# A graph-attention layer: edge weights multiplied into the gathered rows instead of into the one-hot matrices

## The reference, cut to what matters

```
z = (x @ W).reshape(n, HEADS, ODIM)
el = jnp.sum(z * al, axis=-1)
er = jnp.sum(z * ar, axis=-1)
e = jax.nn.leaky_relu(el[src] + er[dst], negative_slope=NEG_SLOPE)
e_max = jax.ops.segment_max(e, dst, num_segments=n)
ex = jnp.exp(e - e_max[dst])
denom = jax.ops.segment_sum(ex, dst, num_segments=n)
alpha = ex / denom[dst]
msg = z[src] * alpha[:, :, None]
out = jax.ops.segment_sum(msg, dst, num_segments=n)
out = out + x.reshape(n, HEADS, ODIM)
out = out + b.reshape(HEADS, ODIM)
out = jax.nn.elu(out)
```

## Time and profile before

| what | value |
|---|---|
| runs | 4824.91, 4829.48, 4825.26 us (median 4825.26) |
| the profiled execution, its span | 4824.0 us |
| PE matmul busy | 3342.4 us, 69% of the span |
| POOL busy | 2537.5 us, 53% |
| DVE busy | 2350.8 us, 49% |
| ACT busy | 1279.2 us, 27% |
| PE's granted clock in both GAT layers | about 0.5 of full speed |

### The profile page before, as it was taken

The page is one execution under the profiler, slowest core; times in us unless marked ns, Lnnn a source line. Parts: engine busy times, 40 slices in busy tenths (PEclk is TensorE's granted clock), DMA queues, the critical chain, the costliest instruction groups (busy, mean ns, idle before and its releaser), DMA issues. The chain is left out here.

```text
span 4824.0 us, 104766 instructions
## 1 busy us (share of the span) xinstructions
PE 3342.4 (69%) x33932; PEld 2406.6 (50%) x33933; DVE 2350.8 (49%) x7219; ACT 1279.2 (27%) x4694; POOL 2537.5 (53%) x2630
## 2 busy tenths in 40 slices
PE   6567766676667775677777776666576776767676
PEld 4334444444444444455555555555455555555555
DVE  6445444444544444445444444444344554444455
ACT  5112211212212212233333333323222222222232
POOL 6444444444444443555555555553655555555553
PEclk9777777777777777555555555555555555555555
DMA  7222222222222222333333333332333333333332
GB/s 231 78 79 83 78 75 80 80 79 81 81 78 81 77 80 84 88 99 94 94 98 93 98 96 94 96 94 75 96 93 102 94 94 94 97 99 93 94 93 82
DMA packets 241750, 442.92 MB, mean 92 GB/s; under 512 B 83665, under 2 KB 134933, under 8 KB 241567
## 3 DMA queue, kind: packets, MB, share of 16 engines
q0 software_dynamic: 119808, 334.13, 25.4%
q1 hardware_dynamic: 121887, 108.14, 7.3%
HBM read 381.95 MB, written 60.10 MB: 92 GB/s over the span
## 5 line engine op out<-in xcount | busy, mean ns | idle before, releaser
L1655 POOL DMA_INDIRECT nodes<-z_rows,scratch x1664 | 1644.4, 988 | 1272.8 <-issue 415.7
L1101 POOL DMA_INDIRECT scratch<-h_rows,scratch x832 | 818.8, 984 | 941.7 <-DVE nodes L1251 716.0
L1732 PE MATMUL ge_part<-nodes,scratch 128*32 128x64 f32 x13312 | 472.6, 313 | 243.2 <-DVE scratch L1927 133.5
L1624 ACT COPY scratch<-ge_part 128x260 f32<-128x260 f32 x208 | 78.3, 376 | 1851.5 <-remote 1665.8
L1145 PE MATMUL ce_part<-nodes,scratch 128*32 128x128 f32 (+1 forms) x6656 | 456.7, 394 | 126.2 <-issue 113.4
L1732 PEld LDWEIGHTS ge_part<-nodes,scratch 128*32 128x32 f32 x13312 | 359.4, 167 | 296.5 <-issue 153.2
L1145 PEld LDWEIGHTS ce_part<-nodes,scratch 128*32 128x32 f32 x6656 | 256.5, 140 | 331.5 <-issue 279.2
L1279 DVE TENSOR_TENSOR nodes<-nodes,ce_sum 128x512 f32 x105 | 72.3, 689 | 707.6 <-remote 367.0
L1737 PE MATMUL ge_part<-scratch 128*32 128x4 f32 x3328 | 209.9, 200 | 261.5 <-issue 259.3
L1746 PE MATMUL ge_sum<-scratch 128*128 128x128 f32 x832 | 243.6, 445 | 208.4 <-ACT scratch L1624 208.2
L1919 DVE TENSOR_TENSOR scratch<-scratch,ge_runs 128x32 f32<-128x32 f32 x208 | 44.0, 212 | 692.4 <-remote 675.5
(11 more groups left out here) (269 smaller groups left out, 5802.1 us busy)
## 6 DMA issues: line engine op xcount, KB each, us to landing
nodes<-z_rows,scratch POOLq DMA_INDIRECT x1664
nodes<-hT SPq DMA_DIRECT2D x56, 256.0 KB
scratch<-h_rows,scratch POOLq DMA_INDIRECT x832
z_rows<-scratch SPq DMA_DIRECT2D x28, 264.0 KB
z_rows<-nodes SPq DMA_DIRECT2D x28, 264.0 KB
hT<-scratch SPq DMA_DIRECT2D x28, 256.0 KB
hT<-nodes SPq DMA_DIRECT2D x28, 256.0 KB
nodes<-x_rows SPq DMA_DIRECT2D x28, 256.0 KB
```

The lines of the kernel that those rows point to most:

```text
L1101: nc.gpsimd.indirect_dma_start(xg[u][:, i * D:(i + 1) * D], None, m.h_rows, bass.IndirectOffsetOnAxis(ap=idx[r][:, k:k + 1], axis=0)).then ...
L1655: nc.gpsimd.indirect_dma_start(zg[r][:, k * ZW:(k + 1) * ZW], None, m.z_rows[layer], bass.IndirectOffsetOnAxis(ap=idx[r][:, k:k + 1], axis ...
L1732: ins = nc.tensor.matmul(ps_part[j * TW:(j + 1) * TW, h * HF:(h + 1) * HF], weighted(k, h), zg[r][:, k * ZW + h * HF:k * ZW + (h + 1) * HF ...
```

## The change

The numerators are written where the gathered row keeps el, which has been read by then: the exponential goes straight into columns 256 to 259 of each tile of `zg[r]`. The 256 columns of each row are then multiplied in place by the row's numerators, head by head: DVE takes the even tiles in one instruction of 1024 elements to a partition and tile 1 in another of 256; ACT takes tiles 3, 5 and 7 in 12 instructions of 64 elements. One matmul per tile then sums 260 columns with the plain one-hot. The buffers `hots` and `ex` go, and with them the waits for `part_summed` (v + 4: the sums of the step before are done with `hots`) ahead of the weighting on DVE and ACT.

```diff
-                nc.scalar.activation(ex[u], diff[u], ACT.Exp).then_inc(ex_ready, 1)
+                nc.scalar.activation(numerators(r), lanes(diff[u]), ACT.Exp).then_inc(ex_ready, 1)
...
-                act.wait_ge(part_summed, v + 4)
                 act.wait_ge(ex_ready, v * 2 + 2)
-                for k in range(G // 2 + 1, G, 2):
+                for k in range(3, G, 2):
                     for h in range(HEADS):
-                        ins = nc.scalar.activation(weighted(k, h), one_hot(r, k), ACT.Copy,
-                                                   scale=ex[u][:, h * (G + 1) + k:h * (G + 1) + k + 1])
-                ins.then_inc(hots_act_ready, 1)
+                        at = k * ZW + D + h
+                        ins = nc.scalar.activation(head_rows(r, k, h), head_rows(r, k, h), ACT.Copy,
+                                                   scale=zg[r][:, at:at + 1])
+                ins.then_inc(rows_act_ready, 1)
...
-                for h in range(HEADS):
-                    for j in range(NB):
-                        k = 2 * j + q
-                        ins = nc.tensor.matmul(ps_part[j * TW:(j + 1) * TW, h * HF:(h + 1) * HF], weighted(k, h),
-                                               zg[r][:, k * ZW + h * HF:k * ZW + (h + 1) * HF],
-                                               start=(q == 0 and h == 0), stop=(q == 1), skip_group_check=True)
                 for j in range(NB):
                     k = 2 * j + q
-                    ins = nc.tensor.matmul(ps_part[j * TW:(j + 1) * TW, D:D + HEADS], one_hot(r, k),
-                                           lanes(ex[r % 2])[:, k, :], start=False, stop=(q == 1), skip_group_check=True)
+                    ins = nc.tensor.matmul(ps_part[j * TW:(j + 1) * TW, 0:D + HEADS], one_hot(r, k),
+                                           zg[r][:, k * ZW:k * ZW + D + HEADS], start=(q == 0), stop=(q == 1),
+                                           skip_group_check=True)
...
+            def scale_rows(r, first, last):
+
+                by_tile = zg[r].rearrange("p (k w) -> p k w", w=ZW)[:, first:last:2]
+                rows = by_tile[:, :, 0:D].rearrange("p k (h f) -> p k h f", h=HEADS)
+                by = by_tile[:, :, D:D + HEADS].rearrange("p k (h o) -> p k h o", o=1)
+                return V.tensor_tensor(rows, rows, by.broadcast_to([P, len(range(first, last, 2)), HEADS, HF]), ALU.mult)
...
                 dve.wait_ge(ex_ready, v * 2 + 1)
-                dve.wait_ge(part_summed, v + 4)
-                weighted_one_hots(r, 0)
-                weighted_one_hots(r, 1).then_inc(hots_ready, 1)
+                scale_rows(r, 0, G).then_inc(rows_scaled, 1)
                 if ahead >= 1:
                     over_tiles(v + 1, 1 - u)
                 scale_first(v - 1, 1 - u, base)
-                weighted_one_hots(r, 0, 1).then_inc(hots_ready, 1)
+                scale_rows(r, 1, 2).then_inc(rows_scaled, 1)
```

More of the change, by code:

```diff
@@ L1405, in gat_stage @@
         hot = [scratch(G * TW) for r in range(4)]
-        hots = scratch(G * HEADS * TW)
         hotT = scratch(2 * P)
@@ L1425, in gat_stage @@
         diff = [scratch(LANES) for u in range(2)]
-        ex = [scratch(LANES) for u in range(2)]
         node = Mem()
@@ L1463, in gat_stage @@
          er_ready, raw_ready, score_ready, eT_ready, ends_ready, lv_ready, state_ready, ini_ready, init_ready, fwd_ready,
-         max_ready, maxT_ready, diff_ready, ex_ready, hots_ready, hots_act_ready, half_summed, part_summed, sums_ready, scaled,
+         max_ready, maxT_ready, diff_ready, ex_ready, rows_scaled, rows_act_ready, half_summed, part_summed, sums_ready, scaled,
          summed, added) = [
@@ L1468, in gat_stage @@
                              "eT_ready", "ends_ready", "lv_ready", "state_ready", "ini_ready", "init_ready", "fwd_ready",
-                             "max_ready", "maxT_ready", "diff_ready", "ex_ready", "hots_ready", "hots_act_ready",
+                             "max_ready", "maxT_ready", "diff_ready", "ex_ready", "rows_scaled", "rows_act_ready",
                              "half_summed", "part_summed", "sums_ready", "scaled", "summed", "added")]
@@ L1480, in one_hot, with numerators, head_rows @@
             return hot[r][:, at:at + TW]
-        def weighted(k, h):
-            at = (k * HEADS + h) * TW
-            return hots[:, at:at + TW]
+        def numerators(r):
+            return zg[r].rearrange("p (k w) -> p k w", w=ZW)[:, :, D:D + HEADS]
+        def head_rows(r, k, h):
+            at = k * ZW + h * HF
+            return zg[r][:, at:at + HF]
         @block.sync
@@ L1722, in tile_sums @@
             def tile_sums(v, r, q):
-                pe.wait_ge(hots_ready, v * 2 + (q + 1))
+                pe.wait_ge(rows_scaled, v * 2 + (q + 1))
                 if q == 0:
@@ L1727, in tile_sums @@
                 else:
-                    pe.wait_ge(hots_act_ready, v + 1)
-                for h in range(HEADS):
-                    for j in range(NB):
-                        k = 2 * j + q
-                        ins = nc.tensor.matmul(ps_part[j * TW:(j + 1) * TW, h * HF:(h + 1) * HF], weighted(k, h),
-                                               zg[r][:, k * ZW + h * HF:k * ZW + (h + 1) * HF],
-                                               start=(q == 0 and h == 0), stop=(q == 1), skip_group_check=True)
+                    pe.wait_ge(rows_act_ready, v + 1)
                 for j in range(NB):
                     k = 2 * j + q
-                    ins = nc.tensor.matmul(ps_part[j * TW:(j + 1) * TW, D:D + HEADS], one_hot(r, k),
-                                           lanes(ex[r % 2])[:, k, :], start=False, stop=(q == 1), skip_group_check=True)
+                    ins = nc.tensor.matmul(ps_part[j * TW:(j + 1) * TW, 0:D + HEADS], one_hot(r, k),
+                                           zg[r][:, k * ZW:k * ZW + D + HEADS], start=(q == 0), stop=(q == 1),
+                                           skip_group_check=True)
                 return ins
```

## The result

The changed kernel takes 4772.64 us (median of 4 runs, 4756.19 to 4807.04) against 4825.09 us: a ratio of 0.9889, 95% interval 0.9847 to 0.9932. It is faster, by 52 us where 295 were forecast. The profiled execution is the slowest of the four, with a span of 4805.3 us: in it the untouched stages ahead of layer 0 took 31 us longer than in the profile before (the first gather of `z_rows` comes at 1934.71 us, before at 1904.05), and from there to the end it is 49 us shorter.

A forecast was written before the change was run, and what follows sets the result against it. Bound: lock-step of POOL's gathers and PE's sums. A step falls from 13.55 to 12.2 us (9.77 of gathers plus a gap); 208 x 1.40 = 291 us off 4824.0 gives 4530 us; range 4190 to 4815, likeliest case 4375 to 4640.

The forecast's parts named there:

- the lock-step of POOL's trains and PE's sums: GAT step: POOL waits for the sums, which are not seen done while POOL issues gathers; 13.5 us per step.
- L1624 at 2628.19 to L1732 at 2632.33 is 4.1 us, plus 0.4 of DVE: Way from ACT's copy to the even half: 4.5 us, so it starts at 2642.2, amid the second four gathers.
- The gap is 2.09 us as now or 2.73 as in the late step: POOL's gap behind eight gathers, read from a present train and one whose second odd gather came late: step 11.9 to 12.5 us.
- 12.2: Forecast time in us of one GAT step, the middle of 11.9 to 12.5, against 13.55 before.
- with 16 instructions I expect ...: Odd half, 16 PE instructions instead of 80: counts as done about 1.2 us after its start, releasing POOL early.
- the lock-step stays: Rival: a half ending inside a block of gathers is held however short it is; 4780 to 4825 us, or 4805; chance 0.16.
- POOL alone is the bound: Rival: neither half is held and POOL never waits; 4105 to 4295 us, most likely 4230; chance 0.24.
- The multiply holds up POOL: Rival, slower: DVE's longer row multiplies stretch or block POOL's gathers; 4908 us, or 5160 for the whole multiply; chance 0.08.
- 0.11 us is all that one multiply cost a gather: Argument against the slower rival: the gather beside the third L1927 takes 1.06 us instead of 0.95.
- The cited queue of 64 entries: TensorE's queue: 80 instructions wait for room, 16 don't; were it the cause, the even half would not be held either.

The follow-up runs named there:

- control: The changed kernel itself, run again on chip 5: 4645.71 us, 0.9832 of the kernel before.
- e1: The changed kernel with the sums of a half in 20 matmuls instead of 4, same columns: 4748.76 us, 1.0039 of the kernel before.
- e7: The changed kernel without the row multiplication but for 2 numbers of each head and one ScalarE activation: 4596.38 us, 0.9723 of the kernel before.
- e12: The kernel before with a POOL pause of 512 numbers ahead of the third gather of each four: 4723.28 us, 0.9986 of the kernel before.
- e8: The changed kernel with each gather replaced by a direct DMA of the same size from fixed places: 3980.73 us, 0.8421 of the kernel before.
- e4: The changed kernel with POOL filling 1024 unused numbers ahead of every four odd gathers: 4566.91 us, 0.9671 of the kernel before.
- e2: The changed kernel with a half's sums in 8 matmuls, 32 instructions instead of 16: 4682.53 us, 0.9896 of the kernel before.

## Why the prediction was wrong, by its own steps

The bound was read rightly: the lock-step of POOL's trains and PE's sums. So were the new pieces: VectorE's multiply 1.21 to 1.23 us (1.21 forecast), ScalarE's 12 activations 2.97 (3.0), the four matmuls 1.10 (1.2), and ScalarE was never late for the odd half in the timelines shown. The odd half counts as done 1.17 us after its start (1.2), and POOL went on without a gap to the eighth gather in 77 of 88 steps of layer 0. A slip of names changed nothing: the four gathers that the prediction calls odd (from 2635.90) are released by the even half and are the even ones.

**The step that failed is "L1624 at 2628.19 to L1732 at 2632.33 is 4.1 us, plus 0.4 of DVE", and with it "The gap is 2.09 us as now or 2.73 as in the late step".** The 4.5 us from ACT's copy to the even half is right for the step that it was read from, r = 2 (4.5 measured), and was taken for all four. That is the one place of a quad in layer 0 that has no work on the nodes in its way. In the other three there is some (in layer 0 PE has a node matmul at r = 0, 2 and 3, three steps of a quad and not two), and the prediction put it at nothing. In the kernel before it cost nothing: the way took 3.3 to 4.1 us on average at every r, and this work fell into the time in which the sums were held anyway. The control shows the way with r = 1, where PE's result is seen at once (L1692 ends at 2638.59):

```profile
2635.58 0.38 ACT L1626 COPY scratch<-ge_part 128x260 f32<-128x260 f32 x1 [6.40 <-issue]
...
2638.74 0.47 DVE L1887 TENSOR_TENSOR_SCAN scratch<-scratch,ge_eT 36x128 f32<-36x128 f32 x1 [2.24 <-PE ge_eT L1692]
...
2639.45 0.67 DVE L1954 TENSOR_TENSOR ge_node<-nodes,ge_node 128x512 f32<-128x512 f32 x1
...
2640.14 0.87 DVE L1957 SCALAR_TENSOR_TENSOR nodes<-nodes,bias,ge_node 128x256 f32<-128x256 f32 x2
...
2640.93 0.68 DVE L1963 COPY nodes<-nodes 128x768 f32 x1
...
2641.54 1.21 DVE L1923 TENSOR_TENSOR nodes<-nodes 128x1024 f32<-128x1024 f32 x1
...
2642.80 1.09 PE L1733 MATMUL ge_part<-nodes,scratch 128*32 128x260 f32 x8 [1.15 <-DVE nodes L1923]
```

7.2 us without any hold, of which VectorE's work on the nodes takes 2.1. In the first comparison a hold of what comes ahead of it is added in 13 of 22 quads (L1692 in the step shown), up to 11.8 us. Where the way is that long, the even half falls behind the train instead of into it, and the gap grows to 3.4 and 5.4 us in layer 0. The gaps of 2.09 and 2.73 us were read at r = 2 and r = 3, and there it measured 2.8 and 1.9.

In numbers, 12.2 was 9.77 us of gathers and a gap of 2.4. In layer 0 the mean gap is 3.4 (1.0 more), in layer 1 it is 2.3, as forecast. The gathers are 0.3 us longer per step in layer 0 and 0.6 in layer 1. Some 0.3 to 0.4 us more go to a gap that is left ahead of the odd four at r = 0 and to the late second gather at r = 2, which the kernel before has too. That makes 13.6 and 13.1: 1.4 and 0.9 us of the forecast gain gone. What each piece of the nodes' work costs no run with it left out shows; that it stands in the way is read from the timelines.

What makes a half held was said as a hunch ("with 16 instructions I expect ..."), and e1 bears it out. I counted PE's MATMUL and LDWEIGHTS records from the start of a train to each result whose consumer is seen waiting, and call it late when the consumer starts over 0.6 us behind the record's end. In the changed kernel 3 of 516 with fewer than 35 records ahead were late, 89 of 106 with 35 to 45, and all 144 with more. There the place would do as well: under 5 us into the train 1 of 514 was late. In the kernel before, all 364 with 70 or more were late, from 1.6 us into the train on, and 20 of 24 with 35 to 45; so it is not the place. But the count isn't sharp either: L1692 is held 4.65 us with 38 records ahead (2646.81), and seen in 0.13 with 42 in another step (2350.59). In e1, 89 of 226 with fewer than 35 were late: after a short gap things are held sooner. It is the instructions since PE was last well supplied, as far as I can tell. A step has some 96 such records (4747 MATMUL and as many loads in the 98.75 steps of the layer 0 window). Had I made the count before, it would have shown that a part of them must be held in a train of eight.

Of the rivals, "the lock-step stays" is nearest in time (4805) and wrong in mechanism; "POOL alone is the bound" fell with the held even half. "The multiply holds up POOL" is there, and its price was read too low: "0.11 us is all that one multiply cost a gather" was read from one gather and a multiply of 256 elements, and beside one of 1024 a gather takes up to 1.3 us more. Since only some gathers meet one, it is 0.2 us per step by e7. The cited queue of 64 entries (Trainium skill, TensorE: Matmul & The Clock Gate, section "Architectural detail: the array is 16× 32×32, not 1× 128×128") would divide 16 from 80 instructions too. But that the even halves then aren't held at all is refuted above: with its 16 instructions, started at 2605.87 inside a train, one released POOL only at 2611.98. What exactly PE lacks in a train, instructions or the way for its signals, stays open: in e1 and e12 its records stretch, which speaks for instructions, and in the changed kernel they go on as if nothing were amiss while its consumers wait.

## What to carry to other kernels

Where one engine issues indirect DMAs back to back, count the instructions that the others must get through meanwhile, not their busy time alone. A short break in the train (here 0.5 us three times a step) gave more than the change itself, but only together with it: on the kernel before, two breaks gave nothing. When a stall is removed, follow the whole chain to the next release, and ask for each link on which side of the new train it will fall. Work that the stall covered comes into the open: where the steps of a loop differ, do this for each of them, and take no figure from one step for all.

## What the runs showed of the hardware that was not expected

- A train of indirect DMAs on GpSimd can hold back what TensorE and SyncE have done or would do, mostly until 0.8 to 1.9 us behind its end. Direct DMAs of the same size from the same engine don't (e8), nor does GpSimd busy with a memset (e4: a result held by the gathers is acted on at 2602.16, before the memset ends at 2602.17).
- By how much depends on the number of PE instructions: at the same columns an odd half of 16, 32 and 80 instructions was seen done 1.25, 2.11 and 3.60 us after its start on average (control, e2, e1).
- The records of PE often don't show it: a matmul that ends at 2646.81 by its record is acted on at 2651.46. Only the consumers' starts do; in e1 and e12 a quarter of the halves show it in PE's records as well.
- A gather beside a multiply of 1024 elements to a partition on VectorE takes up to 2.29 us instead of 0.95; with the multiply left out none takes over 1.2 (e7).
- The same kernel took 4825 us in the first comparison and 4729 to 4732 in three later ones on two chips, and the ratio of the same pair was 0.9889 and 0.9832, with intervals that overlap. Part of the difference lies in stages that the change doesn't touch: the changed kernel's first gather comes at 1934.71 and 1849.26 us. What makes it is not known.
